# Attention scores from six bf16 products, two heads side by side in TensorE's upper and lower 64 rows

## The reference

```python
Q = _rope(split_heads(x @ W_q.T), pos)      # (4, 16, 1024, 8)
K = _rope(split_heads(x @ W_k.T), pos)
score = jnp.einsum('bnqd,bnkd->bnqk', Q, K) / jnp.sqrt(8.0)
score = jnp.where(causal, -jnp.inf, score)  # keys after the query are masked
attn = jax.nn.softmax(score, axis=-1)
out = jnp.einsum('bnqk,bnkd->bnqd', attn, V) @ W_o.T
x = x + ga * out
h = _layernorm(x) * (1 + cb) + sb
x = x + gb * _ffn(h)     # a shared expert and the best 2 of 7 routed experts
```

## Time and profile before

| | us |
|---|---|
| median of 3 runs | 922.52 |
| the three runs | 921.49, 922.52, 930.70 |
| the profiled execution | 927.8 |
| its span (first to last instruction) | 926.1 |
| attention, from quad 0's first L1570 to quad 15's last | 95.8 to 556.9 |
| mean granted TensorE clock over the span | 0.922 |

### The profile page before, as it was taken

The page is one execution under the profiler, slowest core; times in us unless marked ns, Lnnn a source line. Parts: engine busy times, 40 slices in busy tenths (PEclk is TensorE's granted clock), DMA queues, the critical chain, the costliest instruction groups (busy, mean ns, idle before and its releaser), DMA issues.

```text
span 926.1 us, 17554 instructions
## 1 busy us (share of the span) xinstructions
PE 788.9 (85%) x5168; PEld 442.1 (48%) x5168; DVE 625.0 (67%) x1970; ACT 510.4 (55%) x969; POOL 312.4 (34%) x491
## 2 busy tenths in 40 slices
PE   3988999999999999999999997650884778999990
PEld 2551333333333333333333356540764667999880
DVE  5999678998989989998989654720592222333353
ACT  3770366666767666666667778321422444666650
POOL 1347122122111222111221114075014766666562
PEclk9995589999999999999999997795897999999995
DMA  7480311323212332113330195021112222222524
GB/s 200 117 236 23 76 29 26 53 53 53 40 21 47 53 53 53 28 28 53 53 53 3 31 181 117 3 73 41 32 40 60 66 63 65 65 67 65 152 88 142
DMA packets 59051, 62.62 MB, mean 68 GB/s; under 512 B 9097, under 2 KB 50697, under 8 KB 56649
## 3 DMA queue, kind: packets, MB, share of 16 engines
q1 hardware_dynamic: 53218, 50.04, 25.0%
q0 software_dynamic: 4480, 9.64, 2.9%
q10 hardware_dynamic: 1264, 1.84, 0.6%
HBM read 37.55 MB, written 23.55 MB: 66 GB/s over the span
## 4 chain that ended last, share of the span: by engine, by line
PE 66%; DVE 10%; another core or an unknown queue 7%; ACT 6%; issue 5%; DMA 2%; SPq 1%; POOL 1%; ACTq 1%; DVEq 0%; POOLq 0%
PE ps L1492 15%; PE ps L1545 15%; PE ps L1570 14%; PE ps L1726 6%; PE ps L1737 5%; PE ps L1747 2%; DVE junk L1082 2%; PE ps L1633 2%; PE ps L1522 2%; DVE leftmax L1086 1%; PE ps L1641 1%; DMA qa<-mparts 1%; ACT rows L856 1%; SPq L582 1%
## 5 line engine op out<-in xcount | busy, mean ns | idle before, releaser
L835 ACT ACTIVATE probs<-ps 128x1024 f32<-128x1024 f32 (+3 forms) x384 | 295.1, 813 | 181.0 <-PE ps L1570 180.6
L1082 DVE CUSTOM_DVE_ANT_0 junk<-ps,tri 128x128 f32<-128x128 f32 (+3 forms) x512 | 221.6, 486 | 31.0 <-PE ps L1492 28.9
L1492 PE MATMUL ps<-ka,qa 72*128 72x512 bf16 (+3 forms) x768 | 224.1, 348 | 3.6 <-DVE rowmax L1082 2.3
L668 POOL TENSOR_SCALAR_AFFINE_SELECT probs<-probs 128x512 f32<-128x512 f32 x128 | 81.1, 634 | 380.2 <-ACT probs L835 380.2
L1570 PE MATMUL ps<-qa,ka 75*128 75x512 bf16 (+3 forms) x768 | 192.7, 334 | 1.6 <-DMA qa<-mparts 1.5
L1545 PE MATMUL ps<-probs,v 128*32 128x512 f32 (+3 forms) x1536 | 166.5, 506 | 1.8 <-POOL probs L668 1.8
L1086 DVE TENSOR_REDUCE leftmax<-ps 128x1 f32<-128x512 f32 x256 | 162.4, 682 | 7.4 <-PE ps L1492 7.3
L1492 PEld LDWEIGHTS ps<-ka,qa 72*128 72x128 bf16 x768 | 67.2, 99 | 167.6 <-DVE rowmax L1082 65.5
L1570 PEld LDWEIGHTS ps<-qa,ka 75*128 75x128 bf16 x768 | 71.8, 100 | 81.4 <-ACT probs L835 28.8
L735 POOL DMA_INDIRECT routed_results_scratch<-y_s,s_dest x76 | 76.2, 1003 | 61.7 <-issue 56.6
L676 POOL DMA_INDIRECT slot_rows_scratch<-rows,slot x64 | 62.6, 978 | 91.6 <-DVE slot L1283 73.1
(11 more groups left out here) (183 smaller groups left out, 1003.1 us busy)
## 6 DMA issues: line engine op xcount, KB each, us to landing
qa<-q_parts_scratch SPq DMA_DIRECT2D x48, 192.0 KB
slot_rows_scratch<-cst SPq DMA_DIRECT2D x1, 5396.0 KB, 34.3
srow<-slot_rows_scratch SPq DMA_DIRECT2D x76, 71.0 KB
ka<-k_parts_scratch SPq DMA_DIRECT2D x32, 128.0 KB
q_parts_scratch<-qk_parts SPq DMA_DIRECT2D x12, 256.0 KB, 4.6
k_parts_scratch<-qk_parts SPq DMA_DIRECT2D x12, 256.0 KB, 5.4
ka<-k_parts_scratch SPq DMA_DIRECT2D x16, 192.0 KB
xs<-in_x SPq DMA_DIRECT2D x4, 512.0 KB, 10.3
```

The lines of the kernel that those rows point to most:

```text
L668: nc.gpsimd.affine_select(out=p, in_=p, compare_op=ALU.is_ge, fill=0.0, base=0, pattern=[[0, HQ], [1, T]], channel_multiplier=-1).then_inc ...
L835: nc.scalar.activation(probs[s % 4][:, 2 * h:2 * h + 2, 0:CH - q0], ps[:, 2 * h:2 * h + 2, q0:CH], ACT.Exp, scale=SCALE).then_inc(s_exp, 1)
L1082: last = V.tensor_tensor_reduce(out=junk[:, bank - 5, at:at + w], in0=src, in1=tri[:, CH - w:CH], scale=1.0, scalar=LOW, op0=ALU.add, op1= ...
L1492: last = MM(ps[:, bank, at:at + w], qa[m][0:KR, h * S + q * T:h * S + (q + 1) * T], ka[m][0:KR, h * S + k0:h * S + k0 + w], start=True, st ...
```

## The change

The six products of parts whose indices sum to at most two are kept, and three are dropped: the query's parts 0 to 2 against the key's part 0, 0 and 1 against part 1, 0 against part 2 (`RUNS`). The contraction is 48 rows, with the shift 51. Heads 0 and 2 of a quad lie in partitions 0 to 50, heads 1 and 3 in partitions 64 to 114, each with two heads' columns. `load_quad` issues 12 DMAs instead of 8; their rows are 4 KB in two pieces of 2 KB instead of 8 KB, 768 KB in all instead of 1152 KB. `load_shift` issues 6 DMAs of 16 pieces of 256 bytes instead of 3 of 32. The pieces of the maxima alternate between even and odd heads, and the order of the two heads in a pair is chosen so that consecutive matmuls alternate between the upper and the lower rows. Counts of semaphores follow. The ring plan's slots are unchanged.

```diff
 NP = 3
-KR = NP * NP * DK
+RUNS = ((0, NP), (0, 2), (0, 1))
+KR = sum(b - a for a, b in RUNS) * DK
 KM = KR + NP
+HG = 64
+HC = HQ // 2
...
-PIECES = [(h, bank) for h in range(HQ) for bank in HEAD_BANKS]
+PIECES = [(2 * j + g, bank) for j in range(HC) for bank in HEAD_BANKS for g in range(2)]
...
-            qa[m] = sb(f"qa{m}", [KM, HQ * S], BF16, at=att)
-            ka[m] = sb(f"ka{m}", [KM, HQ * S], BF16, at=att)
+            qa[m] = sb(f"qa{m}", [128, HQ * S], BF16, at=att)
+            ka[m] = sb(f"ka{m}", [128, HQ * S], BF16, at=att)
...
             def spill(b):
...
-                        dst = scr[b * NG:(b + 1) * NG, p, :, :].rearrange("g r s -> r g s")
+                        at = NP - 1 - p if w else p
+                        dst = scr[b * NG:(b + 1) * NG, at, :, :].rearrange("g r s -> r g s")
...
             def load_quad(i, r):
                 n, m = quad(i, r), r % 3
...
-                w = NP * DK
-                for j in range(NP):
-
-                    sp.dma_start(qa[m][j * w:(j + 1) * w, :], q[0:w, :]).then_inc(s_qk_in[m], 16)
-                    mid = (j + 1) * w - j * DK
-                    sp.dma_start(ka[m][j * w:mid, :], k[j * DK:w, :]).then_inc(s_qk_in[m], 16)
-                    if j:
-                        sp.dma_start(ka[m][mid:(j + 1) * w, :], k[0:j * DK, :]).then_inc(s_qk_in[m], 16)
+                q = qs_d[n].rearrange("p (d j g) s -> g (p d) j s", j=HC, g=2)
+                k = ks_d[n].rearrange("p (d j g) s -> g (p d) j s", j=HC, g=2)
+                for g in range(2):
+                    at = g * HG
+                    for first, stop in RUNS:
+                        rows_in = (stop - first) * DK
+                        q0, k0 = first * DK, (NP - stop) * DK
+                        dst_q = qa[m][at:at + rows_in, 0:HC * S].rearrange("r (j s) -> r j s", j=HC)
+                        dst_k = ka[m][at:at + rows_in, 0:HC * S].rearrange("r (j s) -> r j s", j=HC)
+                        sp.dma_start(dst_q, q[g, q0:q0 + rows_in, :, :]).then_inc(s_qk_in[m], 16)
+                        sp.dma_start(dst_k, k[g, k0:k0 + rows_in, :, :]).then_inc(s_qk_in[m], 16)
+                        at += rows_in
 
             def load_shift(i, r):
                 m = r % 3
                 sp.wait_ge(s_mparts, quad(i, r) + 1)
-                for p in range(NP):
-                    sp.dma_start(qa[m][KR + p:KR + p + 1, :].rearrange("o (a t) -> o a t", t=T),
-                                 mparts[m][:, p, :]).then_inc(s_m_in[m], 16)
+                for g in range(2):
+                    for p in range(NP):
+                        row = g * HG + KR + p
+                        sp.dma_start(qa[m][row:row + 1, 0:HC * S].rearrange("o (a t) -> o a t", t=T),
+                                     mparts[m][g * HC * TB:(g + 1) * HC * TB, p, :]).then_inc(s_m_in[m], 16)
...
             def row_scores(m, bank, what):
 
                 h, parts = PIECES[what]
+                g0, c0 = h % 2 * HG, h // 2 * S
                 at = 0
                 for q, k0, w, diag in parts:
-                    last = MM(ps[:, bank, at:at + w], qa[m][0:KR, h * S + q * T:h * S + (q + 1) * T],
-                              ka[m][0:KR, h * S + k0:h * S + k0 + w], start=True, stop=True)
+                    last = MM(ps[:, bank, at:at + w], qa[m][g0:g0 + KR, c0 + q * T:c0 + (q + 1) * T],
+                              ka[m][g0:g0 + KR, c0 + k0:c0 + k0 + w], start=True, stop=True)
                     at += w
...
-                pe.wait_ge(s_m_in[m], (third(i, r) + 1) * (16 * NP))
-                ks = [0]
+                pe.wait_ge(s_m_in[m], (third(i, r) + 1) * (16 * 2 * NP))
+                ks, group = [0], [None]
...
                         ring_write(i, r, 5 + ring_bank(i, r, k), kind, off, what)
+                        group[0] = PIECES[what][0] % 2 if kind == "max" else None
                         ks[0] += 1
 
                 for s, (c, kb, q0) in enumerate(STEPS):
-                    for h in range(HQ):
-                        if h % 2 == 0 and not (first and s == 0):
-
-                            pe.wait_ge(s_exp, n * (2 * NS) + 2 * s + h // 2 - 1)
-                        last = MM(ps[:, h, q0:CH], ka[m][0:KM, h * S + kb * T:h * S + (kb + 1) * T],
-                                  qa[m][0:KM, h * S + c * CH + q0:h * S + (c + 1) * CH], start=True, stop=True)
-                        if h % 2:
-                            last.then_inc(s_scores, 1)
-                            ring_entries(s * SLOTS + h // 2)
+                    for pair in range(HC):
+                        if not (first and s == 0):
+                            pe.wait_ge(s_exp, n * (2 * NS) + 2 * s + pair - 1)
+                        for g in ((1, 0) if group[0] == 0 else (0, 1)):
+                            at = pair * S
+                            last = MM(ps[:, 2 * pair + g, q0:CH],
+                                      ka[m][g * HG:g * HG + KM, at + kb * T:at + (kb + 1) * T],
+                                      qa[m][g * HG:g * HG + KM, at + c * CH + q0:at + (c + 1) * CH], start=True, stop=True)
+                            group[0] = g
+                        last.then_inc(s_scores, 1)
+                        ring_entries(s * SLOTS + pair)
```

More of the change, by code:

```diff
@@ L470, in _ @@
             for m in range(3):
-                sp.dma_start(ka[m][KR:KM, :], ones_d.bitcast(BF16)).then_inc(s_ones, 16)
+                for g in range(2):
+                    sp.dma_start(ka[m][g * HG + KR:g * HG + KM, 0:HC * S], ones_d.bitcast(BF16)).then_inc(s_ones, 16)
             def spill(b):
@@ L482, in load_quad @@
                 n, m = quad(i, r), r % 3
-                q = qs_d[bass.ds(n, 1), :, :, :].rearrange("n p (d h) s -> (n p d) (h s)", h=HQ)
-                k = ks_d[bass.ds(n, 1), :, :, :].rearrange("n p (d h) s -> (n p d) (h s)", h=HQ)
-                w = NP * DK
-                for j in range(NP):
-                    sp.dma_start(qa[m][j * w:(j + 1) * w, :], q[0:w, :]).then_inc(s_qk_in[m], 16)
-                    mid = (j + 1) * w - j * DK
-                    sp.dma_start(ka[m][j * w:mid, :], k[j * DK:w, :]).then_inc(s_qk_in[m], 16)
-                    if j:
-                        sp.dma_start(ka[m][mid:(j + 1) * w, :], k[0:j * DK, :]).then_inc(s_qk_in[m], 16)
+                q = qs_d[n].rearrange("p (d j g) s -> g (p d) j s", j=HC, g=2)
[10 more added lines that the diff above has]
+                        at += rows_in
             def load_shift(i, r):
@@ L1077, in bank_maxima @@
                 h, parts = PIECES[what]
+                h = h % 2 * HC + h // 2
                 at = 0
@@ L1500, in ring_write @@
                     if what == 0:
-                        pe.wait_ge(s_qk_in[m], (third(i, r + off) + 1) * ((3 * NP - 1) * 16))
+                        pe.wait_ge(s_qk_in[m], (third(i, r + off) + 1) * (2 * 2 * len(RUNS) * 16))
                     last = row_scores(m, bank, what)
@@ L1525, in _ @@
             pe.wait_ge(s_v_free, 2 * B)
-            pe.wait_ge(s_ones, 16 * 3)
+            pe.wait_ge(s_ones, 16 * 3 * 2)
             for k, (kind, off, what) in enumerate(PRE):
@@ L1798 @@
         cos.astype(np.float32), sin.astype(np.float32), np.eye(128, dtype=np.float32), tri, cst,
-        np.full((NP, HQ * S // 2), 0x3F803F80, np.uint32).view(np.float32),
+        np.full((NP, HC * S // 2), 0x3F803F80, np.uint32).view(np.float32),
     ]
```

## The result

| | before | after |
|---|---|---|
| median on the same chip (4 runs each) | 924.52 us (921.49 to 930.7) | 956.93 us (949.18 to 959.0) |
| profiled execution: time, span | 927.8, 926.1 | 958.79, 957.1 |
| mean granted clock of TensorE | 0.922 | 0.884 |
| attention, first score to last score | 95.8 to 556.9 | 97.3 to 587.2 |
| what stands behind it | 369.2 | 369.9 |

The ratio is 1.0326 with a 95% interval of 1.0243 to 1.041: slower. The forecast was 913.0 with a range of 894 to 936, so the time lies above the range. A ratio here goes over the single runs, without those over 1.5% above the fastest of their kernel, so it differs a little from the quotient of the two medians (1.035 here).

What follows compares the result with a forecast made beforehand. TensorE was taken to set the pace, VectorE only 2.5 us behind per quad. Terms 0.6 - 5 - 2 - 0.2 - 3 = -9.6 gave 918 profiled, 913 us median; range 894 to 936.

Steps and rivals of the forecast that it cites:

- rival (c): TensorE's clock falls in attention because it rests about a quarter of the time; about 980 us, chance 0.07.
- The halves run side by side: Scores and pieces on TensorE: upper and lower rows overlap, nearly all of 7.8 us per quad saved, need about 20.4.
- The switches between scores and transposes: TensorE's tiling mode changes, six a quad at 0.10 us each, an estimated 0.6 us that TensorE can spare.
- (b): Rival: the halves don't overlap and each quad waits for its shift, +0.87 us on 15 boundaries; 935 us, chance 0.13.
- The shift's landing: Shift copies on SyncE's queue: six issues in series land 4.8 us after the first, bounds 3.5 and 5.3.
- (a): Rival: the shift lands in 3.5 to 4.0 us, VectorE's busy time sets the pace; 894 to 902 us, chance 0.22.
- The loads' issues: load_quad on SyncE's queue: 12 issues for 8, 1.2 to 2.4 us more, covered by idle time; no cost.
- The period: Middle quads: 28.0 us each instead of 28.17, 0.15 won on each of 13, 2 us in all.
- Quad 0: First quad of attention, partly at half clock: 5 us won, bounds 10 and 0.
- Opening and the last quads: Opening +0.6 us from the later landing; quad 14 -0.2; quad 15 -3 from half its scores, bounds -3.9 and 0.
- (d): Rival: no change that shows, landing takes 5.3 us and quads 0 and 15 win little; 918 to 926, chance 0.16.

Runs made afterwards that it cites:

- e3: The kernel before with six products in 48 rows in place of nine in 72, without halves; 944.89 us amid four runs far apart, no ratio given.
- e1: The changed kernel with 13 rows of zeros in each half, feeding 61 and 64 rows; 869.81 us, ratio 1.0058 to the kernel before.
- e10: The kernel before with six products and 24 rows of zeros, feeding 72 and 75 rows again; 867.45 us, ratio 1.0011 to the kernel before.
- e4: The kernel before with its three shift copies each cut into two halves, six issues; 891.21 us, ratio 1.0277 to the kernel before.
- e2: The changed kernel with the lower half's three shift copies issued on ScalarE's queue after step 10; 900.55 us, ratio 1.0387 to the kernel before.
- e7: The changed kernel with zero rows, each part of the maxima copied as soon as written; 862.62 us, ratio 0.9949 to the kernel before.
- e6: The changed kernel, unedited, measured again on the other kind of chip; 894.94 us, ratio 1.0283 to the kernel before.
- e11: The changed kernel with the shift two ring entries earlier, no zero rows; 929.24 us, ratio 1.0064 to the kernel before.
- e8: The changed kernel with zero rows and the shift two ring entries earlier; 855.41 us, ratio 0.9858 to the kernel before.
- e9: The changed kernel with zero rows, the shift two ring entries earlier and parts copied as written; 907.73 us, ratio 0.9848 to the kernel before.

## Why the prediction was wrong

**The step that failed is rival (c), the clock.** The forecast had "Clock 1.00 from about 122 to 555", priced a fall at nothing and left (c) outside the range with 0.07. What (c) named as the ground was TensorE's rest, a quarter of the time and 1.7 us ahead of each quad; measured, the usual rest is 0.95 to 1.04, and ten of the 13 falls lie elsewhere. The argument against it was a row in which TensorE was busy 8.82 of 14.50 at full clock. That compared shares of busy time, and what was at work there were mostly matmuls of 128 rows. In its place the runs showed that the clock goes with the rows in use: e3 has TensorE busy 52.02 of 52.02 at 1.2 GHz, and rows of zeros bring the clock back in e1 (one fall of 3.4 us for 13 falls of 85.3, ratio 1.0058 for 1.0283) and in e10. So busy time was the wrong measure to carry over. The prediction itself had said that fewer rows change nothing in a matmul's time, and stopped there; it never asked what 48 rows in place of 72 do to the clock. The Trainium skill (TensorE: Matmul & The Clock Gate, Part 1) says that the gate goes by how busy the engine has been. By busy time alone e3 would have risen early in attention and e10 would equal e3; the runs say otherwise, and they decide.

**The price of (c) was too high.** I had taken 9 us for a quad at half clock and half of the quads, 60 in all (8 times 9 would even be 72). Measured, a spell lasts 3.4 to 10.2 us and not a whole quad. One of 10.2 makes its quad 3.5 longer, one of 3.4 makes it 1.5 to 1.7 longer, two in one quad cost up to 5.6. Six of the twelve middle quads are struck, the half that I had supposed: 21.6 us in quads 2 to 13.

**The halves run side by side: right.** Starts of the two halves within 10 ns of each other, 0.22 for a pair of 512 columns. The switches between scores and transposes, put at 0.10 each and 0.6 a quad, are in no row of their own; the nearest is e3 against e10, 0.35 a quad. So (b) failed for the changed kernel. Its sum for the shift was right in e4 (+0.87 a quad), where its ground, TensorE as the bound, does hold.

**The shift's landing: right.** 4.8 forecast, 4.83 to 5.0 measured, and two late ones of 6.4 and 6.8, which the sum had no term for; they cost 3.6 us. TensorE waits for the landing, 1.04 of it idle here. (a) failed with it: issues of the same line cost 0.59 each whether they carry 32 pieces or 16. (Its low end was added up wrongly as well: 922.5 less 19 and less the 7.6 of the other terms is 896, not 894.) The loads' issues, on the other hand, went from 0.29 to 0.37 each to 0.58 to 0.81, and there are 12 for 8; but no matmul of attention is seen to wait for a load, as argued.

**The period: mis-sized by 0.5.** 28.0 forecast, 28.53 at full clock: +0.36 against before instead of −0.15, +4.7 us over thirteen quads instead of −2. VectorE's wait at the start is 1.79 as forecast (about 1.9), but for all else I had allowed 0.35, and it is 1.14 (28.53 less 25.60 busy and 1.79): 0.43 behind the norm's transposes, 0.29 at the next piece, and further small ones. It was 1.22 before (23.15 less 21.93), so the idle time that I let go hardly went. That both waits belong to short chains through TensorE, which a faster TensorE doesn't shorten, is my reading and not shown.

**Quad 0: right in kind, and larger.** −7.1 for −5: I had taken off 2 us because the clock might rise no earlier, but it rose 8.67 us after the start of attention, before in 26.40. How much of the 7.1 the halves saved is open, and it may be little: in e4, with 75 rows and no halves, the clock rose 11.9 us after the start, and quad 0 took 33.2 in place of 38.7.

**Opening and the last quads.** Start +1.5 for +0.6. Quad 14 was forecast −0.2 and is +2.2, quad 15 −3 and is +1.9; but both had a low clock in part (0.94 and 0.88). With full clock they take 27.0 and 26.3 in e1, +0.7 and −0.7. So the −3 was too much even so: most of the columns saved in quad 15 bring nothing. I had named ScalarE's exponentials for that, but TensorE's weight loads wait 3.3 us in all for them before and in e1 alike, so what holds the quad isn't shown.

**What a range would have had to hold.** With the clock up, e1, the changed kernel is at 1.0058 (1.0024 to 1.0092), some 928 for this chip: (d) in its kind, not the 913 of the forecast. (e1's attention is no longer than that of the profiled run before, 459.0 against 461.1; that run was 5.3 above its median, and no profile at the median was taken, so where e1's 0.6% lies isn't shown.)

**What stays open.** Whether it is the fetched instructions that delay the late landings. Why the clock falls behind a long rest at one quad and not at another. Why e2 has the most spells. Why two halves of 48 and 51 rows rise within 8.67 us in quad 0, where one of 48 and 51 didn't in 232; that both are at work at once there would explain it, but no run tried it alone. Why the clock rises in e4 14 us earlier than in the kernel before.

## What to carry to other kernels

Giving a matmul fewer rows saved none of its time here, and cost the clock of all matmuls around it. When a change takes rows out, or lets TensorE rest in stretches where only matmuls of few rows run, read the granted clock by slice before any busy share, and try rows of zeros, which cost no instruction in the loop here. When an engine stops being the bound, price first the chain that ties the loop's rounds together, here VectorE to copy to TensorE, and ask whether its start can be moved ahead in the queue of the new bound: one number in the plan was worth 1.0 us a quad, twice what the quicker copies of e7 gave. A rare rival whose price is many times the forecast's gain deserves a look at what the row that speaks against it really had at work.

## What the runs showed of the hardware that I had not expected

- Rows of zeros raise TensorE's clock as data does. 48 and 51 rows: 1.2 GHz for 232 us, through the last 205 of them with TensorE busy all the time; 72 and 75 rows, 24 of them zeros: full clock within quad 0, and 1.0011 (0.9968 to 1.0053) of the time before.
- In two halves of 64 rows the same holds: 10 to 17 spells with 48 and 51 rows (the changed kernel, e6, e2, e11), one or two with 61 and 64 (e1, e7, e8, e9).
- 75 rows don't keep the clock up in every case: in e4 it fell three times for 10.2 us, each time behind a rest of 1.59 to 2.66, and never behind the rests of 0.60 to 1.10. But a rest of 2.04 (e1) or 2.41 (e6, e11) went by without a fall.
- A small copy can land late while a packet of 16 KB of instructions is fetched: the shift landed 6.4 and 6.8 us after its first issue in place of 4.8 to 5.0, at the two quads that had such a packet.
- Scores of 51 rows and of 75 beside transposes of 128: 28.53 us a quad in e3, 28.18 in e10, both at full clock.
- A copy of mparts costs 0.59 to 0.62 of its queue whether it holds 32 pieces or 16; on ScalarE's queue three took 1.81, on SyncE's 1.82.
- Chips differ by nearly 7% on this kernel: 922 to 925 and 864 to 866. Attention is the same on both to within a few us (489.9 and 486.8 for the changed kernel); what stands behind it takes 362 to 370 on the one and 310 to 314 on the other.
